# One register load of four block numbers in the maxima step, in place of two loads of two, on VectorE in the graph attention passes

## What is computed

```python
xw = (x @ W).reshape(n_nodes, H, C)                      # H = 8 heads
al_s = jnp.einsum('nhc,hc->nh', xw, a_src)
al_d = jnp.einsum('nhc,hc->nh', xw, a_dst)
logits = jax.nn.leaky_relu(al_s[src] + al_d[dst], 0.2)
m = segment_max(logits, dst)
e = jnp.exp(logits - m[dst])
denom = segment_sum(e, dst)
out = segment_sum((e / denom[dst])[:, :, None] * xw[src], dst)
```

## Time and profile before

| | us |
|---|---|
| median of 3 runs (lowest to highest) | 10514.31 (10507.37 to 10517.66) |
| the profiled execution's own time | 10513.72 |
| its span in the trace | 10511.4 |
| PE, PEld, DVE, ACT, POOL busy | 7135.4, 6194.0, 5278.9, 1896.1, 6605.8 |
| the three softmax passes, first to last `edge_hot` | 1348.6, 1348.3, 1177.4 |

### The profile page before, as it was taken

How to read it: one execution, slowest core, us unless ns; L and a number is a source line. 1 busy time by engine, 2 the same in 40 slices (tenths; PEclk the granted TensorE clock), 3 DMA queues, 4 the chain that set the end, 5 groups by cost and what they waited for, 6 DMA issues and landing times. The chain is left out here.

```text
span 10511.4 us, 139346 instructions
## 1 busy us (share of the span) xinstructions
PE 7135.4 (68%) x31465; PEld 6194.0 (59%) x31466; DVE 5278.9 (50%) x13681; ACT 1896.1 (18%) x4610; POOL 6605.8 (63%) x6850
## 2 busy tenths in 40 slices
PE   0266666666665555547888877888877888688887
PEld 0256565555553444434666655666666777678887
DVE  1233332333332222234777765777756777544444
ACT  0000000000001111112222222222223333222222
POOL 0277775777773777713666634666627777367776
PEclk9855655555556777755666676666665555555555
DMA  0122221222221222203444423444424444244443
GB/s 9 43 58 59 57 59 40 62 59 57 58 54 38 60 60 60 60 21 97 142 141 141 141 85 119 141 141 141 141 64 111 113 111 113 56 116 120 120 120 102
DMA packets 685282, 917.39 MB, mean 87 GB/s; under 512 B 429785, under 2 KB 469403, under 8 KB 685094
## 3 DMA queue, kind: packets, MB, share of 16 engines
q0 software_dynamic: 233472, 500.97, 18.5%
q1 hardware_dynamic: 450726, 414.73, 13.2%
q10 hardware_dynamic: 1024, 1.05, 0.0%
HBM read 899.55 MB, written 17.37 MB: 87 GB/s over the span
## 5 line engine op out<-in xcount | busy, mean ns | idle before, releaser
L1502 POOL DMA_INDIRECT gat_rows<-xw_table,gat_index x2736 | 2590.4, 947 | 1933.8 <-issue 824.6
L1741 PE MATMUL bank<-gat_msg_s,gat_hot 128*128 128x264 f32 (+1 forms) x5472 | 1918.2, 522 | 106.7 <-DVE gat_msg_s L1651 106.6
L1741 PEld LDWEIGHTS bank<-gat_msg_s,gat_hot 128*128 128x128 f32 x5472 | 1394.9, 296 | 377.7 <-issue 110.7
L828 PE MATMUL bank<-gcn_rel,gcn_rhot 100*128 100x64 f32 x3648 | 836.3, 424 | 1019.7 <-DVE gcn_rhot L794 1019.7
L828 PEld LDWEIGHTS bank<-gcn_rel,gcn_rhot 100*128 100x128 f32 x3648 | 794.5, 330 | 1077.2 <-issue 588.3
L683 POOL DMA_INDIRECT gcn_rows<-x_table,gcn_index x912 | 1017.0, 1115 | 276.5 <-issue 257.0
L683 POOL DMA_INDIRECT gcn_rows<-in_x,gcn_index x912 | 1007.7, 1105 | 276.7 <-issue 257.4
L683 POOL DMA_INDIRECT msg_rows<-pre_table,msg_index x912 | 945.9, 1037 | 277.4 <-issue 258.2
L683 POOL DMA_INDIRECT att_rows<-pre_table,att_index x912 | 943.1, 1034 | 276.8 <-issue 254.2
L1719 PEld LDWEIGHTS bank<-gat_ends_s,gat_hot 128*128 128x128 f32 x5472 | 1004.3, 276 | 37.4 <-issue 4.2
L1719 PE MATMUL bank<-gat_ends_s,gat_hot 128*128 128x9 f32 x5472 | 950.1, 312 | 3.3 <-DVE gat_ends_s L1592 3.3
(11 more groups left out here) (293 smaller groups left out, 10442.0 us busy)
## 6 DMA issues: line engine op xcount, KB each, us to landing
gat_dst<-dst_rows SPq DMA_DIRECT2D x342, 512.0 KB
gcn_ids<-rel_rows SPq DMA_DIRECT2D x228, 400.0 KB
att_dst<-dst_rows SPq DMA_DIRECT2D x114, 512.0 KB, 4.0
gat_rows<-xw_table,gat_index POOLq DMA_INDIRECT x2736
att_attr<-in_edge_attr SPq DMA_DIRECT2D x228, 128.0 KB
gcn_rows<-in_x,gcn_index POOLq DMA_INDIRECT x912
gcn_rows<-x_table,gcn_index POOLq DMA_INDIRECT x912
msg_rows<-pre_table,msg_index POOLq DMA_INDIRECT x912
```

Source lines behind the costliest of these rows:

```text
L828: ins = pe.matmul(rel_ps[q][:, j * DIM:(j + 1) * DIM], rhot[q][:, j * P:(j + 1) * P], rel[:, :], start=True, stop=True)
L1502: pool.indirect_dma_start(rows[n.q][:, j, :], None, table, bass.IndirectOffsetOnAxis(ap=index[n.q][:, j:j + 1], axis=0))\
L1741: ins = pe.matmul(sum_ps[g][:, 0:wide], hot[n.q][:, g * GROUP + j, :], msg[q][:, g * GROUP + j, :], start=j == 0, stop=j == GROUP - 1)
```

## The change

`blocks_of` takes a number of groups to load before its own. `maxima` of step n loads the block numbers of steps n-1 and n in one register load (four values), keeps the first two in `earlier` for the adds, which work on step n-1 at that time, and uses the last two itself. The adds load nothing, but for the last step of the pass, which has no `maxima` beside it. The first `maxima` of a pass loads two values, as before.

```diff
-        def blocks_of(eng, n):
-            _, ids = nc.values_load_multi_w_load_instructions(m.block_tab[0:1, n.group(size=PAIR)], engines=[eng.engine],
+        def blocks_of(eng, n, before=0):
+            groups = ds(n.total(PAIR, -before), PAIR + before)
+            _, ids = nc.values_load_multi_w_load_instructions(m.block_tab[0:1, groups], engines=[eng.engine],
                                                               min_val=0, max_val=NB - 1)
             return ids
...
+                earlier = []
+
                 def maxima(n):
                     q = n.of(TWO)
                     view = pick_ps[:, 0:BATCH * (HEADS + 1)].rearrange("p (b h) -> p b h", b=BATCH)
-                    ids = blocks_of(dve, n)
+                    first = n.turn is None and n.total(1, 0) == 0
+                    ids = blocks_of(dve, n, 0 if first else PAIR)
+                    earlier[:], ids = ids[:-PAIR], ids[-PAIR:]
                     dve.wait_ge(picked, n.total(1, TWO + 1))
...
-                ids = []
-
                 def add(g):
                     def part(n):
                         q = n.of(TWO)
-                        if g == 0:
-                            ids[:] = blocks_of(dve, n)
-                        b = ids[g]
+                        b = (earlier or blocks_of(dve, n))[g]
+                        if g == PAIR - 1:
+                            earlier.clear()
```

## The result

| | us |
|---|---|
| before, median (lowest to highest) of 4 runs | 10515.99 (10507.37 to 10518.66) |
| after, median (lowest to highest) of 4 runs | 10408.88 (10405.36 to 10410.54) |
| ratio after / before, 95% interval | 0.9899, 0.9882 to 0.9916 |
| forecast | 10469, range 10380 to 10525 |

The change makes the kernel 107 us faster, 1.0%. The direction was right and the time lies in the range, but the gain is 107 us where the sum has 45, so one of its terms was wrong.

What follows compares the result with a forecast made beforehand. DVE's load gap at the adds was taken as the main bound, with PE and POOL close. Removing 1.16 us and adding 1.00 a step gains 18 us in the third pass and 27 in the others: 10469 us, range 10380 to 10525.

Steps and rivals of the forecast that it cites:

- the sum: Over the three softmax passes: 18 us gained in the third, 27 in the first two, 45 in total.
- What bounds the kernel: Softmax passes: DVE's 1.11 us load gap at the adds, PE second bound in the first two, POOL close in the third.
- What is removed: At the adds: the loads go, so DVE's scaling starts 1.16 us earlier a step.
- What is added: Before `gat_pen` in the maxima: two more loaded values cost 1.03 us, of which 1.00 us becomes new idle time.
- The price of the third and fourth value: In DVE's load at the maxima: 0.233 us each, taken from the difference between one and two values.
- The page's rule: Register loads: about 200 ns a register even in bulk; 0.20 in place of 0.233 would gain 24 us more.
- PE-full steps: First two passes: the 73 of 210 steps that PE fills stay as long as they are.
- (1): Load at the maxima: values three and four come nearly free, 0.63 us a step goes, about 10370 us; chance 0.14.
- (2): First two passes: PE fills more steps at clock 0.50, only the third pass gains, 10496 us; chance 0.18.
- (3): Load at the maxima: third and fourth value cost over 0.30 us each, more than is saved, 10565 us; chance 0.12.
- (4): From maxima to adds: register copies or address arithmetic use up the 0.16 us, about 10500 us; chance 0.06.
- The signs: In the trace: about 345 loads, median near 1.0 us, adds' gap almost none, some 380 us idle before `gat_pen`.

Runs made afterwards that it cites:

- shifted table: The kernel after with its block-number table put 4 bytes further on, so no four-value load starts at a multiple of 16 bytes: 10460.47 us, ratio 0.9944.
- price table: The kernel before with a stage ahead of the attention layers loading 1 to 8 checked values from several table entries: 12954.08 us against 12741.22.
- long runs: Runs, of several kernels of the study, in which every kernel, the unchanged one too, takes 12600 us or more.
- aligned table: The kernel after with a second table so that every four-value load starts at a multiple of 16 bytes, checks kept: 10337.39 us, ratio 0.9826.

## Why the prediction was right or wrong

**What bounds the kernel.** Right. The gap at the adds was DVE's own load and was worth a share of the time; PE fills about a third of the steps in the first two passes (73 before, 69 after, by the cut of the table), and POOL with 10.00 us stands close behind the third, as all kernels with a short load or without checks show: their third pass is at 9.99 to 10.02.

**What is removed, 1.16 us.** Right by what can be seen of it: the idle time at the scaling is 5.7 us, and nothing has taken its place there.

**What is added.** The form is right, and the size for a long load: in the first two passes the idle time that ends with "issue" is 1.06 us behind such a load where 1.00 was taken.

**The price of the third and fourth value: the step that failed.** It was taken as 0.233 us each, from the difference of one and two values. That slope is real: three values cost 741 to 756 ns, and four cost 965 if they begin at another place than a multiple of 16 bytes. But four from a multiple of 16 bytes cost 345 ns in this kernel, and half of the loads are such (171 of the 339 loads of four). The bounds of the sum were -0.60 and +0.15; a short load is outside of them: 345 ns is less than the 536 of two values, which was taken as the least. Its step has the net of -0.16 - 0.63 = -0.79 us, the mean is -0.48.

**The page's rule.** The rule of about 200 ns a register even in bulk ("Runtime: NRT & Kernel Launch" in the Trainium skill, section on instruction fetch mechanics) comes near the long loads (965 / 4 = 241 ns) and fails for the short ones, 86 ns a value. The page speaks of loads out of HBM, the table here lies in SBUF. The other page's floor of about 600 ns ("DMA: Bandwidth & Descriptors", latency and other measured facts) fails for 345 ns as it did for 303. The measurement decides, for both.

**The sum, redone.** This is done with the results at hand, so it shows that the terms fit together, and is no second forecast. Take 0.48 us a step in the first two passes. The prediction let the PE-full steps stay as long as they were; in the table they became 0.15 us shorter (11.85 to 11.70): 228 x (2/3 x 0.48 + 1/3 x 0.15) = 84 us; measured 81.6. In the third pass, steps with a long load lose 0.09 (taken from the shifted table's 10.22) and those with a short one 0.30, down to POOL's 10.0: 22 us; measured 21.7. With the right price the working comes to about 106 us; the passes became 103 us shorter, the kernel 107. With the PE-full steps left as long as they were, as in the prediction, it would be 95. And with all loads long, so with the prediction's own price, the kernel takes 10460 us where 10469 were forecast.

**The PE-full steps.** The commonest length of such a step is 11.69 us, in the kernel before (22 of 73, one of them in the earlier trace rows) and after (54 of 69). But the prediction held all of them as long as they were, up to 12.04 us, and they fell to that length on the mean. In the kernel before they were no longer than the other steps (11.85 against 11.84). One of the kernel after, and the step behind it:

```profile
6909.07:6920.76 11.69, 11.69 (x44) 9.63 (x44) 9.41 (x29) 3.47 (x10) 8.74 (x10) 0.50 0.55 161
6920.76:6931.58 10.82, 7.10 (x45) 5.89 (x43) 9.00 (x28) 3.46 (x10) 7.56 (x8) 0.94 0.54 154
```

**The rivals.** (1), a load costs by the load: half right. It holds for every second load, and for another reason than the one given. With all loads short the kernel takes 10337 us; the rival had 10370, since it put such a load at 536 ns and not at 345. (2), PE takes all of it through a lower clock: fell. The clock rose from 0.68 to 0.74, and is up to 0.79 in the kernels with shorter steps. (3), more than 0.30 us a value: fell. From two values to a long load of four it is (965 - 536) / 2 = 215 ns each. (4), copies eat the gain: fell. DVE's busy time is unchanged, and with all loads as priced the gain is there (58 us).

**The signs.** The number of loads (348 for about 345), the gap at the adds, the third pass at 10.13 and the clock came as written. The median load (528 ns, and no load near it but nine) lies outside of 0.9 to 1.1, and a new wait for PE appeared before `gat_pen`, 177.8 us: both were named as what would refute the prediction, and they do. The second was not in the sum as a term of its own. It was not tried alone; by the timeline it stands where the clock is low: where the pick runs at 1.2 GHz (3.42 us in the place of 1.85) DVE comes before it has ended.

**What stays open.** Why the clock rises where DVE's idle time is moved or taken away was not tried on its own, and how much of the gain of the first two passes comes from the clock is open. Nor is shown why the load from a multiple of 16 bytes is cheap, only that it is.

## What to carry to other kernels

Where a sequencer loads several table values in a step, lay the table out so that each load takes four values from a multiple of 16 bytes behind its start (345 ns in the place of 965), and count 0.28 us of the sequencer more for every value that is checked at run time. Put what is left under the longest instruction of that engine that nothing else waits for, and look for what then becomes late by a tenth of a microsecond. Price a load by measuring it with its size and its place; a slope between two sizes is not the price of a third.

## What the runs showed of the hardware

The price of a register load is not a function of its size alone: 311, 538 and 756 ns for one to three values, 356 for four at a multiple of 16 bytes, 605 for eight; from entry 2, 959 for four and 1854 for eight. In the price table the rounds mostly agree to 10 ns. In the kernels the loads of four have medians near 345 and 965 ns in every trace, the long runs too, and single ones take up to 382 and 1023 ns.

In the long runs the kernel before takes 12741 to 13113 us in the place of 10507 to 10519, with the busy times of the engines within 2% and the same register loads. It is not shown that this belongs to a chip: the record numbers the chips 2, 9 and 11 in these runs, and 2 and 9 again in the later runs in which the kernel before takes 10507 and 10519 us. What differs in the traces is when others learn of PE's work. In the kernel with `messages` ahead of the adds, as a long run (PE's gather, then DVE's instruction that waits for it):

```profile
9306.22 0.48 PE L1731 MATMUL bank<-gat_parts,gat_dhot 128*128 128x48 bf16 x8 [2.32 <-issue]
...
9311.35 0.56 DVE L1635 TENSOR_REDUCE gat_drow<-bank 128x128 f32<-128x384 f32 x1 [4.81 <-remote]
```

PE's gather ends at 9306.70 by the profile, and DVE goes on at 9311.35. In the three softmax passes of this trace 1082 of 2024 signals of PE come over 1 us after the matmul's modelled end, in the kernel before with its 10514 us 22 of 2022. Whether the matmuls end later than the profile shows or their signals travel longer is open. In such runs the aligned table isn't worth anything over the shifted one, so a verdict on 0.5 us of a step should not be taken from them.
